# One decoder layer on one core: the order of the last steps of attention, the last block's queries, and the adds of the expert sums

## The chip, the cores and the metric

The kernel runs as one program on one core of a Trainium2 chip. The metric is the device time of one execution in microseconds (us). The engines are PE (TensorE), DVE (VectorE), ACT (ScalarE), POOL (GpSimd) and SP (SyncE, which only issues DMAs here). Each engine works through its own instructions in order, and semaphores tie them together.

## The reference

Two batches of 1024 tokens of width 256 go through three sublayers, each added to the stream and layer-normalised.

```
q, k, v = x@Wq, x@Wk, x@Wv                      # 16 heads of 64, in sequences of 512
qp, kp  = exp(q@W_feat - |q|^2/2)/sqrt(128), same for k
y_t     = (qp_t . sum_{s<=t} kp_s v_s) / (qp_t . sum_{s<=t} kp_s + 1e-6)
x       = layernorm(x + y@Wo)

att     = softmax(q k / sqrt(8)) over 77 context tokens, 32 half heads of width 8
att     = att[even half] - lam * att[odd half];  x = layernorm(x + att@v)

scores  = sigmoid(x@gate_w.T); choose 2 of 4 groups, then 4 of 16 experts
w       = chosen scores / their sum * 2.5
x       = layernorm(x + sum_e w_e * down_e(silu(gate_e x) * up_e x) + shared(x))
```

## The kernel before

**Blocks.** The 2048 tokens are four blocks of 512 (`NBLK` = 4, `NT` = 4 column tiles of 128). A Python list of jobs, `schedule()`, is made once; every engine's program walks the same list and issues its own part of each job, so the list is the order of the work on every queue. `merged(main, extra)` lays a second list evenly into a first. A job that an engine has no part in costs it nothing.

**Attention.** Steps t = 0 to 67 run the linear attention, 16 heads per block (`attention_jobs`). Beside them, `chain_jobs(b, s)` puts the rest of block b's layer at s = t - 16(b+1): output projection and first norm (s = 4), queries (5), scores (7, 8), probabilities and their weighing with the context values (10 to 14, the second norm at the end of 14), transposes and gate (15), routing and the shared expert (16 to 18), scatter of the rows to their experts' regions in DRAM (19, job `dispatch`: 16 indirect DMAs that POOL issues). For the third block these steps are t = 52 to 67, the end of attention. With its dispatch come `ends` and `table` (L1272 to L1288), small DVE steps that count how many tiles of 128 rows each expert has; `pack` (L1731 to L1733, L1451) turns the result into registers' worth of numbers that SP, PE and ACT read.

**Last block.** The last block (`DENSE`) can't wait for a dispatch, so all 16 experts are computed for all of its tokens ("dense"). Its output projection, first norm, transposes (`turn stream`, L1630) and queries stand between attention and the tile loop. A query job (L1506 with `w_xq` as the stationary side) makes 128 of the 256 query columns for 512 tokens in 6 matmuls of 512 columns: 3 passes of high and low halves in f16, times 2 halves of the inner size. ACT copies the high part (L994), DVE makes the low part (L1362), and SP then moves the pieces with 12 DMAs (L748) into `xq`, whose partitions 0 to 31 hold the high part, 32 to 63 the low part and 64 to 95 the high part again for 4 half heads of each of 8 groups. A score job is one matmul of 96 partitions (L1648) and one maximum on DVE (L1367), 32 in all.

**Tile loop.** Steps 0 to 36 run 32 pairs of tiles of the other three blocks: rows in (SP, L790), transposes (`tile turn`, L1726), gate and up matmuls (`tile up`), down matmuls (`tile down`), and POOL's two scatters of the results (L907). Into each step's jobs goes a part of the last block's chain (`gaps`): scores in steps 1 to 7, the maxima in 8, 24 probability jobs and 16 weighing jobs in 9 to 16, the second norm in 17, transposes and gate in 19, routing and shared expert in 20 and 21, weights in 22. From step 24 on every second step has the jobs of one dense expert.

**A dense expert.** `dense_jobs(e)` is gate e, up e, weigh e-1, keep e-1, down e-2. In time: ACT's tanh (L1068), two DVE products (L1461, L1465), one DVE product with the weights (L1471), ACT's high part (L1073), POOL's low part (L912), PE's down matmuls. The tanh of expert e+1 waits for POOL's low part of expert e-1.

**Last stage.** The dense experts that are left are merged with 12 sums: SP fetches a token's four expert rows into one of three buffers (`fetch`, L802), and `combine` (L1484 to L1486) adds them pairwise, adds the result to the total, and takes the statistics (L1177, L1178). After four of them comes the third norm of that block (`norm3`; the rows are scaled on ACT, L1077). The last block's own totals and norm end the program.

## Time and profile before

| | us |
|---|---|
| median of 3 runs (lowest, highest) | 1026.03 (1025.96, 1027.13) |
| profiled execution, its own time | 1016.03 |
| its span, first to last instruction | 1014.0 |
| PE busy | 843.3 (83%) |
| DVE busy | 658.9 (65%) |
| ACT busy | 498.0 (49%) |
| POOL busy | 349.8 (34%) |

The span is 2.03 us shorter than the execution's own time, and that is 10.0 us (1.0%) under the median of the timed runs. Busy shares are means over stages that differ; the windows among the rows below give each stage by itself. In every view times count from the span's start, and a line's number is that of the code above.

### The profile page before, as it was taken

The numbers are of one execution on the slowest core, as the hardware profiler recorded it, in microseconds if no ns is written. First come the engines' busy times: TensorE is split into PE (matmuls) and PEld (weight loads), VectorE is DVE, ScalarE is ACT, GpSimd is POOL, SyncE is SP. The second block draws the span as 40 slices with busy tenths as digits, with TensorE's granted clock in tenths as the row PEclk, the third lists the DMA queues.
The fourth block names the chain that finished last, engine by engine and source line by source line (L and its number), as shares of the span: only waits on it lengthen the run. The fifth ranks groups of instructions, "written<-read, shape, count | busy, mean of one in ns | idle before, by whom it ended". The sixth has DMA issues, their size and how long they took to land.

```text
span 1014.0 us, 19634 instructions
## 1 busy us (share of the span) xinstructions
PE 843.3 (83%) x6908; PEld 628.4 (62%) x6908; DVE 658.9 (65%) x1714; ACT 498.0 (49%) x1003; POOL 349.8 (34%) x376
## 2 busy tenths in 40 slices
PE   5899969999789898999889889886577787699753
PEld 2578757766566676767667667665355565576432
DVE  4676644567566955776694576568366666764888
ACT  4777656344565435367443437720125763454221
POOL 4211111001781171079116105912304672355121
PEclk9999998999999999899989989987778997899986
DMA  8466666131121232011033221242533222332341
GB/s 294 106 169 185 136 129 181 34 81 33 34 54 34 64 131 58 21 32 44 22 83 114 60 78 32 73 172 95 167 91 112 79 89 68 110 99 97 122 153 75
DMA packets 70157, 96.64 MB, mean 95 GB/s; under 512 B 19632, under 2 KB 50480, under 8 KB 69552
## 3 DMA queue, kind: packets, MB, share of 16 engines
q1 hardware_dynamic: 64688, 79.92, 27.7%
q0 software_dynamic: 5376, 15.47, 4.2%
q8 instruction: 59, 0.97, 0.4%
q14 instruction: 34, 0.28, 0.1%
HBM read 42.33 MB, written 33.10 MB: 74 GB/s over the span
## 4 chain that ended last, share of the span: by engine, by line
PE 47%; DVE 24%; ACT 8%; issue 7%; POOL 6%; SPq 4%; DMA 3%; ACTq 0%; DVEq 0%
PE ps L1506 22%; PE ps L1603 4%; POOL prob L885 4%; PE ps L1606 4%; PE ps L1584 4%; PE ps L1593 3%; SPq L688 2%; PE ps L1574 2%; PE ps L1575 2%; PE ps L1576 2%; DVE xmax L1367 1%; PE ps L1563 1%; PE ps L1648 1%; POOL low_parts L878 1%; DVE st L1177 1%
## 5 line engine op out<-in xcount | busy, mean ns | idle before, releaser
L878 POOL TENSOR_TENSOR low_parts<-square,qk 128x512 f16<-128x512 f32 x64 | 76.0, 1188 | 414.3 <-DVE qk L1314 414.3
L1312 DVE SCALAR_TENSOR_TENSOR low_parts<-ps,qk 128x512 f16<-128x512 f32 x64 | 44.2, 690 | 107.6 <-ACT square L969 104.5
L885 POOL TENSOR_TENSOR prob<-prob_full,prob 128x512 f16<-128x512 f32 x84 | 101.3, 1231 | 6.1 <-ACT prob_full L1007 5.6
L964 ACT ACTIVATE qk<-ps 128x512 f16<-128x512 f32 x64 | 38.1, 596 | 131.7 <-PE ps L1506 131.7
L907 POOL DMA_INDIRECT rows_out<-attn_mem,dest x64 | 62.4, 975 | 101.3 <-ACT attn_mem L1058 86.8
L1506 PE MATMUL ps<-x_split,w_qkv 128*128 128x512 f16 x384 | 94.4, 383 | 0.9 <-DVE low_parts L1312 0.9
L1603 PE MATMUL ps<-attn_mem 128*128 128x65 f32 x512 | 92.2, 272 | 2.1 <-issue 2.1
L1603 PEld LDWEIGHTS ps<-attn_mem 128*128 128x128 f32 x512 | 80.1, 195 | 10.2 <-issue 3.3
L1606 PE MATMUL ps<-run,attn_mem 128*128 128x65 f32 x384 | 75.0, 277 | 0.0
L1584 PE MATMUL ps<-attn_mem 128*128 128x128 f32 x512 | 74.2, 291 | 0.0
L980 ACT ACTIVATE attn_mem<-ps 128x512 f32<-128x512 f32 x64 | 38.3, 599 | 70.1 <-PE ps L1576 69.4
L1584 PEld LDWEIGHTS ps<-attn_mem 128*128 128x128 f32 x512 | 67.6, 203 | 1.7 <-DVE xmax L1367 0.3
L1593 PEld LDWEIGHTS ps<-attn_mem 128*128 128x128 f32 x448 | 62.2, 203 | 9.5 <-ACT square L969 1.5
L1506 PE MATMUL ps<-xv,prob 128*128 128x68 f16 x1152 | 46.2, 195 | 21.9 <-POOL prob L885 19.0
L1506 PE MATMUL ps<-attn_mem,w_qkv 128*128 128x128 f16 x512 | 60.4, 236 | 4.3 <-DVE x_mem L1393 3.3
L900 POOL DMA_INDIRECT rows_in<-rows,slot_i x48 | 46.5, 969 | 50.5 <-DVE slot_i L1267 36.4
L1593 PE MATMUL ps<-attn_mem 128*128 128x65 f32 x448 | 61.9, 281 | 1.4 <-ACT square L969 1.2
L1007 ACT ACTIVATE prob_full<-ps 128x512 f32<-128x512 f32 x96 | 59.7, 622 | 6.1 <-POOL prob L885 4.9
L1506 PEld LDWEIGHTS ps<-xv,prob 128*128 128x128 f16 x1152 | 43.1, 99 | 30.8 <-issue 23.2
L1574 PE MATMUL ps<-qk,w_feat_high 128*128 128x512 f16 x128 | 50.3, 393 | 12.7 <-DMA qk<-low_parts 12.3
L1367 DVE TENSOR_REDUCE xmax<-ps 128x4 f32<-128x308 f32 x128 | 53.0, 469 | 10.1 <-PE ps L1648 10.1
L1606 PEld LDWEIGHTS ps<-run,attn_mem 128*128 128x128 f32 x384 | 59.0, 194 | 0.0
(284 smaller groups left out, 2122.4 us busy)
## 6 DMA issues: line engine op xcount, KB each, us to landing
qk<-low_parts SPq DMA_DIRECT2D x128, 128.0 KB, 2.4
attn_mem<-rows_in SPq DMA_DIRECT2D x64, 144.0 KB, 2.2
late_mem<-ffn_w SPq DMA_DIRECT2D x17, 384.0 KB, 3.6
rows_in<-zero_row SPq DMA_DIRECT2D x32, 144.0 KB, 2.2
up_split<-late_mem SPq DMA_DIRECT2D x16, 256.0 KB, 3.4
xq<-late_mem SPq DMA_DIRECT2D x48, 64.0 KB, 2.0
x_stage<-xT SPq DMA_DIRECT2D x4, 512.0 KB, 4.7
down_split<-late_mem SPq DMA_DIRECT2D x16, 128.0 KB, 3.6
```

What stands on the lines that cost most here:

```text
L878: pool.tensor_tensor(low_parts[:, n % 2, 1, :], square[:, n % 2, :], qk[:, n % 2, n // 2 % 2, 0, 1, :], ALU.subtract).then_inc(p_sql.sem, 1)
L885: pool.tensor_tensor(prob[:, n % RING, 1, :], prob_full[:, n % FULL, :], prob[:, n % RING, 0, :], ALU.subtract).then_inc(pr_low.sem, 1)
L900: pool.indirect_dma_start(rows_in[GROUP_OF[b]], bass.IndirectOffsetOnAxis(ap=slot_i[:, b, j:j + 1], axis=0), row_mem[:, b % 2, j // TOPK, ...
L907: pool.indirect_dma_start(rows_out[b], bass.IndirectOffsetOnAxis(ap=dest[:, i % YB, j:j + 1], axis=0), yb[:, i % YB, j, :], None).then_inc ...
L1007: act.activation(prob_full[:, n % FULL, :], bank[:, :], ACT.Exp, scale=float(XD) ** -0.5).then_inc(pr_exp.sem, 1)
L1367: dve.tensor_reduce(xmax[:, c, GH * g:GH * g + GH], bank[:, 0:GN].rearrange("p (j n) -> p j n", j=GH), AX.X, ALU.max).then_inc(sc_max.sem, 1)
L1506: ins = pe.matmul(dst, lhs(i), rhs(j), start=first and n == 0, stop=last and n == 2)
L1574: pe.matmul(bank[:, :], w_feat_high[:, :], source[:, 0, :], start=True, stop=False)
L1584: last = pe.matmul(bank[:, t], kf[:, n % 2, t], qf[:, n % 4, t], start=True, stop=True)
L1593: last = pe.matmul(bank[:, V1 * c:V1 * c + V1], kt[:, n % 2, c, :], v1[:, c, n, :], start=True, stop=True)
L1603: last = pe.matmul(o, att[:, (H * b + n) % 3, c, :], v1[:, c, n, :], start=True, stop=not before)
L1606: last = pe.matmul(o, qf[:, n % 4, P * c:P * c + P], held, start=False, stop=True)
```

## The change

1. For the third block the steps of `chain_jobs` are drawn together: the second norm goes from s = 14 to the end of 13, everything behind it one step forward, routing parts 2 and 3 and the prefix sums into one step, so dispatch, `ends` and `table` go from t = 67 to t = 65 and `pack` from behind two output projections to t = 66. The first two blocks keep their steps.
2. The first `rows in` jobs go ahead of the last block's output projection. The last block's transposes go from ahead of the loop into step 1, its queries into steps 2 to 7, mixed with the scores. POOL spreads the query weights beforehand (job `spread wxq`, t = 63, 6 copies of 128x512 f16) as high, low, high columns for each group of 4 half heads; 8 query jobs then make 96 rows each, in the layout of `xq`, and the 12 DMAs are gone. ACT copies all 96 rows, DVE subtracts on rows 32 to 63.
3. Scores of the last block run group by group. Its second norm goes to the end of step 16, transposes and gate to 18, routing and shared expert to 19 to 22, weights to 23. Dense expert 0's gate and up go into step 21, and the dense jobs from step 24 on are each one expert further.
4. Of the three adds of a `combine` the first two go from DVE to POOL; DVE waits for them.

```diff
-    if 10 <= s <= 14:
-        for n in range(6 * (s - 10), min(6 * (s - 9), CHUNKS)):
+    if 10 <= s <= 13:
+        for n in range(6 * (s - 10), 6 * (s - 9)):
...
+    tail = [weighs(b, CHUNKS - 1) + [("norm2", b, 0)],
+            several("turn cross", range(2)) + several("gate", [0]),
+            several("route", [0]) + several("shared up", range(2)) + several("route", [1]),
+            several("route", [2]) + several("shared down", range(2)),
+            several("route", [3]) + several("prefix", [0]),
+            several("dispatch", [0]) + several("keep", [0])]
+    if closing:
+        tail[-1] += [("ends", GROUP_OF[b], 0), ("table", GROUP_OF[b], 0)]
+        tail = [tail[1], tail[2], tail[3] + tail[4], tail[5], [("pack", GROUP_OF[b], 0)]]
+        if s == 13:
             jobs += weighs(b, CHUNKS - 1) + [("norm2", b, 0)]
...
+def last_chain():
...
+    gaps[1] = several("turn stream", range(2))
+    part = []
+    for g in range(NG + 1):
+        if g < NG:
+            part += several("queries", [g])
+        if g:
+            part += several("scores", range(NT * (g - 1), NT * g))
+    spread(part, 2, 6)
+    gaps[8] = several("turn maxima", [0])
...
+    spread(part + weighs(DENSE, CHUNKS - 1), 9, 8)
+    gaps[16] += several("norm2", [0])
+    gaps[18] = several("turn cross", range(2)) + several("gate", [0])
+    gaps[19] = several("route", [0]) + several("shared up", range(2))
+    gaps[20] = several("route", [1])
+    gaps[21] = several("route", [2]) + several("shared down", range(2)) + dense_jobs(0)
+    gaps[22] = several("route", [3])
+    gaps[23] = several("weights", [0])
...
-    out_parts = chain[4]
-    jobs += out_parts[:2] + [("pack", 0, 0)] + out_parts[2:]
     for step in range(-3, 0):
         jobs += tile_jobs(0, step)
-    jobs += chain[5]
+    jobs += [("project out", DENSE, n) for n in range(NT)] + [("norm1", DENSE, 0)]
...
+                elif kind == "spread wxq":
+                    pool.wait_ge(*weighed(b - 1, 2 * NG))
+                    for part in range(2):
+                        for copy in range(3):
+                            pool.tensor_copy(w_xq3[...], w_xq[...]).then_inc(wxq_spread.sem, 1)
+                elif kind == "combine":
+                    i = NT * b + n
+                    four = yg[i % YG]
+                    pool.wait_ge(*yg_loaded[i % YG](i // YG + 1, 0))
+                    pool.tensor_tensor(four[:, 0:2, :], four[:, 0:2, :], four[:, 2:4, :], ALU.add).then_inc(paired.sem, 1)
+                    pool.wait_ge(*paired(i, 1))
+                    pool.tensor_tensor(four[:, 0, :], four[:, 0, :], four[:, 1, :], ALU.add).then_inc(paired.sem, 1)
...
+                elif kind == "queries" and b == DENSE:
+                    dve.wait_ge(*xq_high(b, n + 1))
+                    dve.scalar_tensor_tensor(xq[32:64, n, :], bank[32:64, :], 1 / W_SCALE, xq[32:64, n, :], ALU.mult,
+                                             ALU.subtract).then_inc(xq_low.sem, 1)
...
-                    dve.wait_ge(*yg_loaded[i % YG](i // YG + 1, 0))
+                    dve.wait_ge(*paired(i + 1, 0))
                     four = yg[i % YG]
-                    link(dve.tensor_tensor(four[:, 0:2, :], four[:, 0:2, :], four[:, 2:4, :], ALU.add))
-                    link(dve.tensor_tensor(four[:, 0, :], four[:, 0, :], four[:, 1, :], ALU.add))
                     dve.tensor_tensor(total[:, n, :], four[:, 0, :], total[:, n, :], ALU.add).then_inc(folded.sem, 1)
```

## Rows read from the trace of the kernel before

**Rows 1.** Windows: length, busy us by engine (instructions), granted clock, DMA share, GB/s.

```profile
664.00:702.40 38.40, 26.01 (x219) 22.75 (x215) 30.73 (x102) 7.42 (x13) 0.91 (x2) 0.81 0.21 81
702.40:740.20 37.80, 20.80 (x124) 14.44 (x125) 14.87 (x52) 2.88 (x5) 15.39 (x16) 0.68 0.53 171
740.20:766.70 26.50, 25.04 (x229) 18.84 (x230) 21.68 (x52) 10.78 (x30) 4.63 (x5) 0.89 0.32 98
...
835.50:877.00 41.50, 26.29 (x248) 21.79 (x249) 30.88 (x86) 14.70 (x44) 11.36 (x12) 0.79 0.24 74
877.00:933.60 56.60, 56.52 (x509) 39.68 (x508) 33.24 (x61) 31.34 (x94) 31.41 (x33) 1.00 0.29 94
...
938.60:1010.90 72.30, 42.81 (x214) 23.09 (x213) 61.80 (x152) 16.40 (x29) 12.56 (x10) 0.82 0.31 112
```

**Rows 2.** Timeline of PE around the tile loop's start: start, us, [idle before <-releaser].

```profile
703.13 8.01 PE L1506 MATMUL ps<-w_o,yT 128*128 128x256 f16 x48 [2.71 <-DVE yT L1345]
...
721.23 1.94 PE L1630 MATMUL ps<-ident,rows 128*128 128x128 f32 x8 [4.54 <-DVE rows L1194]
724.68 4.87 PE L1506 MATMUL ps<-late_mem,w_xq 128*128 128x512 f16 x12 [1.50 <-DVE late_mem L1358]
729.38 0.60 PE L1726 MATMUL ps<-ident,attn_mem 128*128 128x128 f32 x4
740.21 0.67 PE L1648 MATMUL ps<-xk,xq 96*128 96x308 f16 x2 [10.23 <-issue]
```

**Rows 3.** Timeline of DVE from the third block's second norm on.

```profile
667.34 0.42 DVE L1177 BATCH_NORM_STATS2 st<-rows 128x6 f32<-128x256 f32 x1
...
702.22 0.17 DVE L1267 CAST slot_i<-slot_f 128x16 int32<-128x16 f32 x1
702.30 0.68 DVE L1345 TENSOR_TENSOR yT<-ps,yT 128x512 f16<-128x512 f32 x1
...
706.42 0.16 DVE L1288 TENSOR_TENSOR row_n<-row_n,tile_f 128x1 f32<-128x1 f32 x1
```

**Rows 4.** Timelines of POOL and of SP: last dispatch, rows in, queries' DMAs.

```profile
721.67 0.96 POOL L900 DMA_INDIRECT rows_in<-rows,slot_i  x1 [0.30 <-issue]
...
725.06 3.59 SPq L790 DMA_DIRECT2D attn_mem<-rows_in  x6
730.98 7.72 SPq L748 DMA_DIRECT2D xq<-late_mem  x12
```

**Rows 5.** One line's instructions: duration ns min/median/max, first and last start.

```profile
L1362 DVE SCALAR_TENSOR_TENSOR late_mem<-ps,late_mem x2: 692/692/692, 728.1 to 730.2; 128x512 f16<-128x512 f32 x2
...
L912 POOL TENSOR_TENSOR prob<-prob x16: 1147/1251/1472, 894.4 to 995.9; 128x512 f16<-128x512 f32 x16
```

**Rows 6.** Timeline of POOL: one operation with one input, one with two.

```profile
11.22 3.55 POOL L870 TENSOR_SCALAR_AFFINE_SELECT xk<-xk 128x2464 f16<-128x2464 f16 x1
...
665.25 0.46 POOL L890 TENSOR_TENSOR x_mem<-x_mem 128x128 f32<-128x128 f32 x1 [2.60 <-DVE x_mem L1393]
```

**Rows 7.** Timelines of ACT, POOL and DVE in the last stage.

```profile
943.30 0.63 ACT L1073 ACTIVATE prob<-prob 128x512 f16<-128x512 f32 x1 [3.45 <-DVE prob L1471]
...
944.01 1.33 POOL L912 TENSOR_TENSOR prob<-prob 128x512 f16<-128x512 f32 x1 [4.85 <-ACT prob L1073]
...
943.18 0.69 DVE L1484 TENSOR_TENSOR square<-square 128x512 f32<-128x512 f32 x1
943.90 0.42 DVE L1485 TENSOR_TENSOR square<-square 128x256 f32<-128x256 f32 x1
944.36 1.26 DVE L1486 TENSOR_TENSOR yT<-square,yT 128x256 f32<-128x256 f32 x1
945.65 0.43 DVE L1177 BATCH_NORM_STATS2 st<-yT 128x6 f32<-128x256 f32 x1
...
946.21 0.65 DVE L1461 SCALAR_TENSOR_TENSOR prob<-prob,ps 128x512 f32<-128x512 f32 x1
...
961.36 0.69 DVE L1461 SCALAR_TENSOR_TENSOR prob<-prob,ps 128x512 f32<-128x512 f32 x1 [2.62 <-ACT prob L1068]
```

More of the change, by code:

```diff
@@ L1 @@
+import collections
 from contextlib import ExitStack
@@ new lines, in chain_jobs, with several, spread @@
+    if closing:
+        tail[-1] += [("ends", GROUP_OF[b], 0), ("table", GROUP_OF[b], 0)]
+        tail = [tail[1], tail[2], tail[3] + tail[4], tail[5], [("pack", GROUP_OF[b], 0)]]
+        if s == 13:
+            jobs += weighs(b, CHUNKS - 1) + [("norm2", b, 0)]
+    if 14 <= s < 14 + len(tail):
+        jobs += tail[s - 14]
+    return jobs
+def last_chain():
+    def several(kind, ns):
+        return [(kind, DENSE, n) for n in ns]
+    gaps = collections.defaultdict(list)
+    def spread(part, first, steps):
+        per = -(-len(part) // steps)
+        for i in range(steps):
+            gaps[first + i] += part[per * i:per * (i + 1)]
+    gaps[1] = several("turn stream", range(2))
[7 more added lines that the diff above has]
+    gaps[8] = several("turn maxima", [0])
+    part = []
+    for n in range(CHUNKS):
+        part += [("probs", DENSE, n)]
+        if n >= 3:
+            part += weighs(DENSE, n - 3)
+    spread(part + weighs(DENSE, CHUNKS - 1), 9, 8)
[6 more added lines that the diff above has]
+    gaps[23] = several("weights", [0])
+    return gaps
@@ L191, in schedule @@
             jobs.append(("experts", 0, 1))
-    chain = {step: chain_jobs(DENSE, step) for step in range(4, 19)}
-    out_parts = chain[4]
-    jobs += out_parts[:2] + [("pack", 0, 0)] + out_parts[2:]
+            jobs.append(("spread wxq", DENSE, 0))
     for step in range(-3, 0):
         jobs += tile_jobs(0, step)
-    jobs += chain[5]
-    gaps = {}
-    def spread(parts, first, steps):
-        part = [j for p in parts for j in p]
-        per = -(-len(part) // steps)
-        for i in range(steps):
-            gaps[first + i] = part[per * i:per * (i + 1)]
-    spread([chain[7], chain[8]], 1, 7)
-    gaps[8] = chain[9]
-    spread([chain[step] for step in range(10, 15)], 9, 9)
-    for i, step in enumerate((15, 16, 17, 18)):
-        gaps[19 + i] = chain[step]
-    dense = [dense_jobs(e) for e in range(NE + 2)]
-    done = 0
+    jobs += [("project out", DENSE, n) for n in range(NT)] + [("norm1", DENSE, 0)]
+    gaps = last_chain()
+    done = 1
     for step in range(0, PAIRS_OF[0] + DOWN + 1):
-        extra = gaps.pop(step, [])
-        if step >= 23 and step % 2 == 0:
-            extra = extra + dense[done]
+        extra = gaps[step]
+        if step >= 24 and step % 2 == 0:
+            extra = extra + dense_jobs(done)
             done += 1
@@ L226, in schedule @@
             ahead[i + 2].append(("norm3", bb, 0))
-    rest = [job for part in dense[done:] for job in part]
+    rest = [job for e in range(done, NE + 2) for job in dense_jobs(e)]
     jobs += merged(rest, [job for part in ahead for job in part])
@@ L742, in _ @@
                         load_context(b // BLK_PER_BATCH)
-                elif kind == "queries" and n == KD - 1:
+                elif kind == "queries" and b != DENSE and n == KD - 1:
                     sp.wait_ge(*xq_high(b, KD))
```

47 lines of the change are left out of this document (27 added, 20 removed).

## The prediction

> **What bounds the kernel now.** I read the windows by stage first, then the timelines at the stages' edges, then single lines. The windows' edges are: the third block's last weighing, its slots ready, step 1 of the tile loop, step 8, the last block's second norm, step 24, the last scatter landed, the first sum fetched, the end. In [rows 1] each stage has its own bound. 664 to 702: DVE, 30.7 of 38.4 us busy. 702 to 740: nothing, PE works 20.8 of 37.8 us at a granted clock of 0.68; the largest gap is 10.23 us before the first score [rows 2], in which SP takes 7.72 us to issue the queries' DMAs [rows 4]. 740 to 767, steps 1 to 7: PE, 25.0 of 26.5. 835 to 877: DVE, 30.9 of 41.5. 877 to 934: PE, 56.5 of 56.6. The last 72.3 us: DVE, 61.8. POOL has 12.6 us of work there, which invites the move of two adds. Whether they may go depends on what stands around them in POOL's and DVE's queues, and that is where I expect the change to lose.
>
> **Third block's chain.** The second norm starts at 667.34 [rows 3], when POOL's last add on the stream is through, issued at 665.25 [rows 6] and followed by a second of the same kind. Moved into t = 61 it still needs this add, and the weighing in front needs POOL's low parts as before. Only one head's output, 0.75 us of DVE, no longer stands ahead of it, and the weighing moves little, as PE puts that head's matmuls between its two halves: the norm begins about 1.1 us sooner. Against that, POOL now makes its six weight copies at once behind that add. No copy is in the trace. Below: 0.5 us each. Above: 1.25, the two-input low part of 512 columns (L912, median [rows 5]). I take 0.75, by the nearest one-input row, 3.55 us for 2464 columns [rows 6], with some start cost: 4.5 us, on an idle POOL. They cost DVE about 1 us where they collide with the norm's small two-input steps (the collision is shown below). So the norm ends when it did. From there to the slots (702.22) DVE keeps the same routing, but work of t = 65 and 66 falls behind them: a state, an output, another output, a transpose's low part, 2.9 us; work of t = 62 comes in, 2.1 us. Net the slots come at about 701.4, 0.8 us sooner, in a range of 3 sooner to 1 later.
>
> Behind the slots the order turns against the last block. Today the table's 3.5 us of small steps (to 706.42) lie under the output projection, which started at 703.13 [rows 2, 3]. Now they stand in DVE's queue before the last head's output, `pack` and the last transposes. From the slots on: state 0.7, low part 0.7, output 0.75, `ends` 0.15, table 3.65, output 0.75, `pack` 0.3, transposes on PE 0.7, ACT's copy 0.6, low part 0.7, together 9.0. The projection starts at 710.4 instead of 703.1 and runs to 724.0 (13.6 as before: 703.13 to 716.7, the 4.54 idle before 721.23 taken off it [rows 2]). The norm behind it takes those 4.5 us: 728.5.
>
> **Tiles from the end of attention.** POOL's 16 dispatches end at 722.6 today and the rows are fetched at 725.06 [rows 4]; they move with the slots, to 724.3, and the first tile can be turned at about 726.9. Step 1 is then at 727.8 instead of 740.7, and the 10.23 us gap is gone. Late next is the first query: transposes 728.6 to 730.5, ACT's and DVE's parts to 731.8.
>
> **Queries made in place.** Eight jobs of 6 matmuls instead of two, none outside the loop. 12 matmuls took 4.87 us at the low clock level [rows 2]; at the high one a 512-column matmul is half, 0.216, so a job is 1.3 us and eight are 10.4. DVE pays 8 x 0.6 (L1362 spans 0.69 [rows 5] and overlaps the next by a tenth), ACT 8 x 0.6. SP loses 7.7 us of issues. This work lies in steps 2 to 7, where PE is full: its 25.0 us of steps 1 to 7 [rows 1] less one turn, plus 10.4, is 34.3. DVE there has 21.7 + 4.8 = 26.5, so it doesn't bind. With 2 us of waits for the ACT-DVE handover of each query and for the clock after the idle, step 8 begins at 731.8 + 36.3 = 768.1. It began at 766.7: **+1.4 us**. Ends: without those waits and with slots 2 us sooner -2.6; with 1.2 us of handover exposed at each query and the low clock for the first two, +8.
>
> **Steps 8 to 24.** Steps 8 to 16 are the same. The norm at the end of step 16 waits for the same POOL add, while DVE's 2.1 us of step 17, done in that wait today, fall behind it. DVE bounds until step 24 and gets 1.3 us more for dense expert 0. Against these 3.4 us stand its 10.6 us idle of 41.5 [rows 1], of which the wider spread and a filled PE may return some 3: **+0.5**, from -3 to +4.
>
> **Steps 24 to 36.** PE is full, and one expert's selection (0.3) and down matmuls (12 x 0.11) join: **+1.6**, from 0 to +2.
>
> **Two adds on POOL.** On DVE they cost 0.72 + 0.46 per sum, start to start, and the third with its statistics 0.46 + 0.56 [rows 7]: 2.2 us x 12 = 26.4. The trace also shows why it is dearer: L1486 started at 944.36 under POOL's low part (944.01 to 945.34) and took 1.26 instead of 0.43 [rows 7]. Eight or nine of the 12 sums meet this once, +0.83 each: 33.5 in all. DVE further waits 2.62 twice for ACT, which scales rows for the norm (961.36 is one [rows 7]), 0.5 for a fetch, and has one expert (three products, 2.0) more to do than after the change, as that one has moved into step 21 to 36: 41.2 us.
>
> After: POOL's two adds. No 512-column f32 add is in the trace. Below: DVE's own 0.69 + 0.42; above: twice the 1.33 of [rows 7]. I take 1.2 + 0.7 + the handover 0.1 = 2.0, from the low part (512 columns) and the 0.46 for 128 columns [rows 6]. The merge gives DVE this order: up 8, weigh 7, sum 0, up 9, weigh 8, sum 1, up 10, sum 2, weigh 9, sum 3, up 11, norm, weigh 10, sum 4, up 12, weigh 11, sum 5, up 13, sum 6, weigh 12, sum 7, norm, up 14, weigh 13, sum 8, up 15, weigh 14, sum 9, weigh 15, sum 10, sum 11. POOL has: low part 7, adds 0, low part 8, adds 1 and 2, low part 9, adds 3, low part 10, adds 4 and 5, low part 11, adds 6, low part 12, adds 7, low part 13, adds 8 and 9, low part 14, adds 10, low part 15, adds 11. So for sums 1, 3, 4, 7 and 8 DVE has just made the product from which ACT makes the high part (0.63 + 0.1), from which POOL makes the low part (1.15 at its shortest [rows 5], + 0.1), and only then POOL adds (2.0): DVE stands still 3.9 us, with the next expert queued behind it and PE behind that. The waits: 2.0, 3.9, 0, 3.9, 5.2 (the ACT scaling sits in front), 0, 0, 3.8, 3.8, 0, 2.1, 2.6 = 27.3. At four of the sums that follow, POOL has begun the next operation when DVE's add is released: 1.1 each, 4.4. One wait for a tanh, 1.5. The third adds and statistics, 12.0. Sum 45.2 against 41.2: **+4.0**, from 0 (adds of 1.6, no collisions) to +7. The fetches stay covered: a buffer is free some 10 us before its next use, a load took 5.0 (933.6 to 938.6, two edges of [rows 1]).
>
> In a sentence the rest can do without: the Trainium skill, SBUF — State Buffer, "SBUF: two separate sides", calls the ports that DVE and POOL share an exclusive lock that the operation that starts first keeps to its end; the trace agrees (1.26 against 0.43), but by that rule DVE's add may also win the race at the four places, which would take 3.3 us off the sum. And its GPSIMD Engine Reference, "Elementwise — side-by-side cycle accounting", gives 4497 ns for an add of 2048 f32 columns on GpSimd; an estimate from that page is 1.7 us for both adds, by which the last stage would be +2.2 instead of +4.0.
>
> **The sum.** 1.4 + 0.5 + 1.6 + 4.0 = +7.5 us on the profiled execution's 1016.03 (span 1014.0 and 2.03 around it), so 1023.5 there. The timed median is 10.0 above that execution; I carry the difference over: 1026.03 + 7.5 = 1033.5.
>
> **Rivals.**
> - *The front pays.* If the slots come 4 us sooner (DVE's gaps in its 38.4 us close) or the table's steps slip into waits, the first query is at 726 and step 8 at 762, -4.6; routing spread wider gives -2.5; +1.6; the last stage at its lower half +1.5. Together -4, 1022. For it: 7.7 us DVE idle in the first window [rows 1] and the gap of 10.23. Against: the slots hang on POOL's add and a serial routing.
> - *DVE is freed.* If DVE reached its adds late enough that POOL had always finished, 26.4 + 7.1 would shrink to 12: the stage would fall onto the dense experts' own cycle, about -10, in all -6.5, 1019.5. Against: the order of the two queues above. It is the faster side's cheapest case and turns on that one point.
> - *The loop gets latency-bound.* Each query in steps 2 to 7 passes PE, ACT, DVE and then scores, and the DVE chain of the tiles shares the queue. If 1.2 us shows for each query, the low clock stays for two, and the middle gives +3: +14, 1040.
> - *It cancels,* within 2 us: every term near its lower end but none below.
>
> **Chances.** Forecast (+2 to +11) 0.50, front pays 0.12, DVE freed 0.10, latency-bound 0.20, cancels 0.08. The measurement can tell 0.2%, 2 us: faster 0.22, same 0.08, slower 0.70. The likeliest case by itself reaches from 1028 to 1037; with half of the faster cases and most of the slow one the range is 1021 to 1041.
>
> **What would show it.** After the change: POOL's six copies right behind the last stream add and under 6 us together; slots at 699 to 703; output projection at 708 to 712; the DMAs of L748 gone for the last block and no PE gap over 4 us before the first score; 8 query jobs of 1.3 us; step 8 at 764 to 772; in the last stage DVE's waits before its one add in two kinds, near 4 us and near nothing, released by POOL; L1486 at 1.26 where POOL works. I am wrong if those waits sum to less than 15 us, or if step 8 comes before 762.

## The result, and the profile after

The changed kernel took 1032.56 us (median of 11 runs, 1025.53 to 1037.57); the kernel before took 1024.05 in the same rounds (median of 11, 1017.63 to 1028.58). The ratio is 1.0081, 95% interval 1.005 to 1.0112: slower by 8.3 us, from 5.1 to 11.5. The forecast was 1033.5, +7.5. Here and below medians are over all executions, while ratios and intervals leave out those more than 1.5% above the fastest of the same kernel; e2's profile (1032.79) is of one that they leave out.

The profiled execution took 1032.56, its span is 1030.5, against 1016.03 and 1014.0. These 16.5 us are not all the change's: 9.7 of them are there before any changed instruction runs (the last block's attention begins at 522.1 instead of 512.4, with the same code in front of it; in e1 to e4, with that code too, it begins at 512.3 to 522.8). From that point on the span is 6.9 us longer, and that is what the rows below divide.

Windows of the changed kernel, with the stages' own edges (columns as in [rows 1]): the second norm of the third block to its slots; slots to step 1; steps 1 to 7; steps 8 to 16; steps 17 to 23; steps 24 to 36; the first sum's load; the last stage.

```profile
671.60:709.85 38.25, 27.97 (x210) 24.35 (x209) 29.45 (x95) 7.91 (x14) 3.56 (x7) 0.76 0.19 73
709.85:737.17 27.32, 19.70 (x136) 16.90 (x136) 14.22 (x57) 1.19 (x2) 15.54 (x16) 0.75 0.59 202
737.17:777.71 40.54, 35.63 (x282) 24.66 (x281) 30.70 (x64) 16.71 (x40) 5.80 (x6) 0.93 0.28 81
777.71:843.10 65.39, 47.80 (x625) 37.50 (x623) 40.31 (x76) 44.31 (x116) 39.62 (x44) 0.91 0.26 79
843.10:890.71 47.61, 34.91 (x321) 26.76 (x319) 34.55 (x97) 17.50 (x55) 15.09 (x16) 0.87 0.26 80
890.71:948.72 58.01, 57.94 (x516) 40.34 (x514) 34.29 (x61) 31.74 (x95) 32.71 (x33) 1.00 0.27 89
948.72:953.88 5.16, 4.79 (x27) 2.47 (x26) 1.97 (x3) 1.23 (x2) 1.62 (x2) 1.00 0.81 289
953.88:1030.50 76.62, 40.17 (x187) 21.05 (x187) 41.25 (x125) 15.24 (x27) 32.92 (x33) 0.75 0.31 111
```

Three of the stages of the kernel before, cut at the same events (slots to step 8, steps 8 to 16, steps 17 to 23), and its last stage from the first fetch's issue on:

```profile
702.39:766.65 64.26, 45.79 (x353) 33.23 (x354) 36.51 (x105) 13.65 (x35) 19.97 (x21) 0.77 0.44 141
766.65:830.94 64.29, 47.52 (x625) 37.64 (x623) 40.79 (x77) 44.57 (x116) 39.77 (x45) 0.92 0.29 89
830.94:877.04 46.10, 30.72 (x303) 25.40 (x300) 33.73 (x94) 16.87 (x50) 15.28 (x18) 0.81 0.26 79
933.67:1013.99 80.32, 47.50 (x240) 25.47 (x238) 63.79 (x155) 17.63 (x31) 13.95 (x11) 0.82 0.35 125
```

Slots to step 8 takes 27.3 + 40.5 = 67.9 instead of 64.3; steps 8 to 16, 65.4 instead of 64.3; 17 to 23, 47.6 instead of 46.1; 24 to 36, 58.0 instead of 56.6; the last stage 5.2 + 76.6 = 81.8 instead of 80.3, although DVE is busy in it for 43.2 us instead of 63.8.

PE at the loop's start, to be laid beside [rows 2], and POOL's weight copies:

```profile
719.29 12.14 PE L1555 MATMUL ps<-w_o,yT 128*128 128x256 f16 x96 [1.50 <-DVE yT L1392]
735.72 0.81 PE L1785 MATMUL ps<-ident,attn_mem 128*128 128x128 f32 x4 [4.29 <-DMA attn_mem<-rows_in]
...
740.69 2.76 PE L1555 MATMUL ps<-late_mem,prob 128*96 128x512 f16 x12 [1.61 <-DVE late_mem L1405]
```

```profile
671.78 3.39 POOL L944 COPY prob<-w_xq 128x512 f16<-128x512 f16 x6
```

The projection starts 9.50 us behind the slots (709.79) instead of 0.74, the 10.23 us gap before the first score has become one of 1.61 before the first query, and the first two query jobs, 12 matmuls, are 2.8 us of PE. In the last stage, POOL's queue and DVE's:

```profile
952.77 1.15 POOL L956 TENSOR_TENSOR prob<-prob 128x512 f16<-128x512 f32 x1 [3.54 <-ACT prob L1120]
953.88 1.27 POOL L951 TENSOR_TENSOR x_stage<-x_stage 128x512 f32<-128x512 f32 x1
955.23 0.72 POOL L953 TENSOR_TENSOR x_stage<-x_stage 128x256 f32<-128x256 f32 x1
959.86 1.15 POOL L956 TENSOR_TENSOR prob<-prob 128x512 f16<-128x512 f32 x1 [3.91 <-ACT prob L1120]
960.97 1.26 POOL L951 TENSOR_TENSOR square<-square 128x512 f32<-128x512 f32 x1
962.31 0.73 POOL L953 TENSOR_TENSOR square<-square 128x256 f32<-128x256 f32 x1
963.00 1.26 POOL L951 TENSOR_TENSOR low_parts<-low_parts 128x512 f32<-128x512 f32 x1
```

```profile
958.44 0.68 DVE L1522 TENSOR_TENSOR prob<-prob,ps 128x512 f32<-128x512 f32 x1
963.08 1.47 DVE L1535 TENSOR_TENSOR yT<-square,yT 128x256 f32<-128x256 f32 x1 [3.96 <-POOL square L953]
...
966.50 0.42 DVE L1535 TENSOR_TENSOR yT<-low_parts,yT 128x256 f32<-128x256 f32 x1
...
972.13 0.42 DVE L1535 TENSOR_TENSOR yT<-x_stage,yT 128x256 f32<-128x256 f32 x1 [3.95 <-POOL x_stage L953]
```

Read the two queues together. DVE ends its product at 959.12, ACT makes the high part of it (0.6), POOL the low part from 959.86 to 961.01, and only then come the two adds, to 963.04; DVE had nothing else to do. POOL makes the adds of sum 2 right behind (to 965.13), and DVE, which comes to that sum at 966.50, takes it without a wait. Over the stage, who waited for whom (us, times, longest):

```profile
DVE yT L1535 <- POOL square L953: 15.2, 4, 5.4
DVE yT L1535 <- POOL x_stage L953: 8.3, 3, 4.0
DVE yT L1535 <- POOL low_parts L953: 5.5, 3, 4.0
```

### The profile page after: what moved, and what is told of

Read it like the earlier page. It is cut to its first block, busy times and chain, and to the rows that moved or that the text cites. A ratio compares the mean times of both kernels' runs of the same rounds, so it can differ in the third digit from the quotient of the medians.

```text
span 1030.5 us, 19735 instructions
## 1 busy us (share of the span) xinstructions
PE 860.9 (84%) x6944; PEld 637.0 (62%) x6944; DVE 644.9 (63%) x1696; ACT 501.5 (49%) x1009; POOL 376.0 (36%) x406
## 4 chain that ended last, share of the span: by engine, by line
PE 46%; DVE 22%; POOL 11%; ACT 8%; issue 6%; SPq 5%; DMA 2%; ACTq 0%; POOLq 0%; DVEq 0%
PE ps L1555 22%; PE ps L1652 4%; POOL prob L915 4%; PE ps L1655 4%; PE ps L1633 3%; SPq L718 3%; PE ps L1642 3%; DVE xmax L1418 2%; PE ps L1623 2%; PE ps L1624 2%; PE ps L1625 2%; POOL rows_in L930 1%; PE ps L1612 1%; POOL low_parts L908 1%; POOL prob L956 1%
## 5 line engine op out<-in xcount | busy, mean ns | idle before, releaser
L1652 PE MATMUL ps<-attn_mem 128*128 128x65 f32 x512 | 96.6, 282 | 2.3 <-issue 2.1
L1555 PE MATMUL ps<-x_split,w_qkv 128*128 128x512 f16 x384 | 97.3, 391 | 1.0 <-DVE low_parts L1359 1.0
L1655 PE MATMUL ps<-run,attn_mem 128*128 128x65 f32 x384 | 78.4, 288 | 0.0
L1633 PE MATMUL ps<-attn_mem 128*128 128x128 f32 x512 | 71.8, 284 | 0.0
L1024 ACT ACTIVATE attn_mem<-ps 128x512 f32<-128x512 f32 x64 | 38.3, 599 | 68.7 <-PE ps L1625 67.9
L1555 PE MATMUL ps<-xv,prob 128*128 128x68 f16 x1152 | 47.3, 198 | 27.3 <-POOL prob L915 25.6
L930 POOL DMA_INDIRECT rows_in<-rows,slot_i x48 | 46.7, 972 | 48.9 <-DVE slot_i L1314 34.9
L1642 PE MATMUL ps<-attn_mem 128*128 128x65 f32 x448 | 61.7, 280 | 1.4 <-ACT square L1013 1.2
L1655 PEld LDWEIGHTS ps<-run,attn_mem 128*128 128x128 f32 x384 | 62.4, 204 | 0.0
L1623 PE MATMUL ps<-qk,w_feat_high 128*128 128x512 f16 x128 | 50.3, 393 | 13.6 <-DMA qk<-low_parts 13.2
L1555 PE MATMUL ps<-w_qkv,x_split 128*128 128x512 f16 x192 | 51.7, 417 | 11.1 <-DVE w_qkv L1150 11.1
```

Source lines behind the costliest of these rows:

```text
L930: pool.indirect_dma_start(rows_in[GROUP_OF[b]], bass.IndirectOffsetOnAxis(ap=slot_i[:, b, j:j + 1], axis=0), row_mem[:, b % 2, j // TOPK, ...
L1555: ins = pe.matmul(dst, lhs(i), rhs(j), start=first and n == 0, stop=last and n == 2)
L1623: pe.matmul(bank[:, :], w_feat_high[:, :], source[:, 0, :], start=True, stop=False)
L1633: last = pe.matmul(bank[:, t], kf[:, n % 2, t], qf[:, n % 4, t], start=True, stop=True)
L1642: last = pe.matmul(bank[:, V1 * c:V1 * c + V1], kt[:, n % 2, c, :], v1[:, c, n, :], start=True, stop=True)
L1652: last = pe.matmul(o, att[:, (H * b + n) % 3, c, :], v1[:, c, n, :], start=True, stop=not before)
```

## The experiments

Twelve runs in three sets of four. A set ran on one chip with its own runs of the kernel before: median 1021.32 in the first, 1063.12 in the second, 1061.88 in the third. So ratios are compared, and stages only between profiles of like chips. "Slots to step 8" and the like are lengths between the same events in every kernel.

**e1, the adds on DVE again.**

```diff
 # POOL: kind "combine" removed; DVE, kind "combine":
-                    dve.wait_ge(*paired(i + 1, 0))
+                    dve.wait_ge(*yg_loaded[i % YG](i // YG + 1, 0))
                     four = yg[i % YG]
+                    link(dve.tensor_tensor(four[:, 0:2, :], four[:, 0:2, :], four[:, 2:4, :], ALU.add))
+                    link(dve.tensor_tensor(four[:, 0, :], four[:, 0, :], four[:, 1, :], ALU.add))
```

> The changed kernel with all three adds of a sum back on DVE, everything else as changed. Theory (POOL's adds stand behind the low parts and DVE waits for them: 27 us of waits against 26 us of adds and collisions saved): the last stage, from the first fetch's issue to the end, goes back from 81.8 to about 80 us, so this kernel is 1 to 3 us faster than the changed one and still 5 to 8 us slower than the kernel before. Rival (the POOL adds are the main loss): it comes back to within 2 us of the kernel before. Rival (they do free DVE): it is 3 us or more slower than the changed kernel.

Measured: 1019.71, ratio 0.9993 (0.9958 to 1.0028). The whole loss is gone with the adds: not the theory but its first rival, the adds as the main loss, held, and the last stage took 73.3 us where about 80 were expected. Windows of its last stage, the first sum's load and the rest up to DVE's last norm:

```profile
941.27:945.94 4.67, 4.43 (x26) 2.37 (x25) 1.98 (x4) 1.23 (x2) 1.13 (x2) 1.00 0.80 281
945.94:1011.43 65.49, 37.23 (x188) 19.82 (x187) 58.04 (x149) 15.24 (x27) 11.12 (x9) 0.80 0.35 124
```

From the first add to the end of DVE's work: 65.5 us here, 73.5 in the changed kernel (953.88 to 1027.41), 72.3 before (938.59 to 1010.86). DVE's busy time and its gaps of over 0.3 us in the three: 58.0 and 2.8; 41.3 and 28.2; 61.8 and 5.7. So the adds on POOL save DVE 16.8 us of work and cost it 25.4 of waiting, +8.0 with the gaps below 0.3 us counted too. And the other edit that reaches this stage, one expert moved out of it, is worth 6.8, not the 2.0 of its three products alone. Besides them DVE has two stretched operations fewer (an add, 1.26 instead of 0.42, and a norm step, 1.00 instead of 0.16; 1.7 together) and 2.9 us less of gaps.

**e2, the two adds one place earlier in the merge.**

```diff
-        ahead[i + 2].append(("combine", bb, c))
-        if c == NT - 1:
-            ahead[i + 2].append(("norm3", bb, 0))
+        ahead[i + 2].append(("pair", bb, c))
+        ahead[i + 3].append(("combine", bb, c))
+        if c == NT - 1:
+            ahead[i + 3].append(("norm3", bb, 0))
```

> The changed kernel, but DVE's part of each sum is put one sum later in the list than POOL's two adds, so that POOL has finished when DVE comes to it. Same work on every engine. Theory (the order of the two queues costs it, not the adds' length): DVE's waits for POOL in the last stage fall from 29 us to under 6, and the stage falls from 81.8 us by 10 to 16, to the cycle of a dense expert (4.7 us) or PE. The kernel is then 2 to 8 us faster than the kernel before. Rival (POOL's adds collide with DVE and delay the low parts, whatever the order): the stage falls by less than 4 us.

Measured: 1029.94, ratio 1.0052 (1.0009 to 1.0094). By the medians, 1029.94 and 1021.32, it would be 1.0084. Last stage 78.1 instead of 81.8: 3.7 us, where the theory wanted 10 to 16 and its rival less than 4, so this run alone speaks for the rival. DVE still waits 19.0 us for POOL (under 6 expected), and now for ACT as well:

```profile
DVE yT L1536 <- POOL square L954: 10.7, 3, 5.4
DVE prob L1513 <- ACT prob L1116: 8.8, 4, 3.0
DVE yT L1536 <- POOL x_stage L954: 7.0, 2, 4.0
```

One place in the merged list moved most pairs from one side of DVE's jobs to the other, but not past the low part in POOL's queue. e7 does that.

**e3, the last block's queries by DMA again** (the two 128-column jobs, placed by SP, all of them ahead of step 2, and scores in steps 4 to 7).

```diff
-    part = []
-    for g in range(NG + 1):
-        if g < NG:
-            part += several("queries", [g])
-        if g:
-            part += several("scores", range(NT * (g - 1), NT * g))
-    spread(part, 2, 6)
+    gaps[1] += several("queries", range(KD))
+    spread(several("scores", range(NT * NG)), 4, 4)
```

> The changed kernel with the last block's queries made as before (2 jobs of 6 matmuls, 12 DMAs by SP), now in step 1 of the tile loop, and the 32 scores in steps 4 to 7; no weight copies on POOL. Theory (PE is full in steps 2 to 7, and the 36 added matmuls cost 7.8 us there one for one): PE's busy time up to step 8 falls by 7 to 8 us, the DMAs hide behind tile work in steps 2 and 3, and step 8 begins 4 to 7 us sooner than in the changed kernel; the kernel is 4 to 7 us faster than the changed one. Rival (the DMA way's 10 us gap was the cost, the matmuls fill idle time): PE stands still 5 us or more before the first score, and the kernel is no faster than the changed one.

Measured: 1031.29, ratio 1.008 (1.0046 to 1.0113), as the change. Slots to step 8: 67.1 (711.46 to 778.59) against 67.9. The DMA's way is still there, 8.0 us of issues from 747.0 on SP. What PE waited for in steps 0 to 7:

```profile
PE ps L1684 <- DMA xq<-late_mem: 7.4, 1, 7.4
```

PE works 5.2 us less than in the change (50.2 of 67.1 against 55.4 of 67.9), and stands 7.4 us in one gap instead. So the rival held: step 8 came 0.8 us sooner behind the slots, not 4 to 7. Making the queries in place gained nothing by itself.

**e4, the table and pack behind the first part of the projection's stage.**

```diff
-        tail[-1] += [("ends", GROUP_OF[b], 0), ("table", GROUP_OF[b], 0)]
-        tail = [tail[1], tail[2], tail[3] + tail[4], tail[5], [("pack", GROUP_OF[b], 0)]]
+        tail[-1] += [("ends", GROUP_OF[b], 0)]
+        tail = [tail[1], tail[2], tail[3] + tail[4], tail[5]]
...
+    jobs += [("table", 0, 0)] + [("project out", DENSE, n) for n in range(2)] + [("pack", 0, 0)]
     for step in range(-3, 0):
         jobs += tile_jobs(0, step)
-    jobs += [("project out", DENSE, n) for n in range(NT)] + [("norm1", DENSE, 0)]
+    jobs += [("project out", DENSE, n) for n in range(2, NT)] + [("norm1", DENSE, 0)]
```

> The changed kernel with the tile table computed behind the last head's output and the last transposes (beside the output projection, where it was before), the rest of the third block's chain as changed. Theory: the output projection starts 4 to 4.5 us sooner, but the first tiles still wait for the dispatched rows and stand ahead of the last block's transposes in PE's queue, so the first query starts only 0 to 1.5 us sooner; total 0 to 2 us faster than the changed kernel. Rival (the projection's late start is what delays the queries): first query and end are 4 us sooner.

Measured: 1033.04, ratio 1.0119 (1.0079 to 1.016). The projection started 8.4 us behind the slots instead of 9.5, 1.1 sooner where 4 to 4.5 were expected, and PE then stood for the first rows, so that the first query came 30.8 us behind the slots instead of 30.9:

```profile
735.19 1.09 PE L1786 MATMUL ps<-ident,attn_mem 128*128 128x128 f32 x4 [4.91 <-DMA attn_mem<-rows_in]
```

The table is not what holds the projection; the last head's output and transposes, which the drawn-together chain leaves behind the slots, are. That this run is 0.4% above the change is within the two intervals and not explained by its stages (slots to step 8 is 66.5), and I leave it open.

**e5, adds on DVE and the third block's chain as before** (on the second chip).

```diff
 # closing block: "ends" and "table" stay behind "keep", nothing else is drawn together
-        tail = [tail[1], tail[2], tail[3] + tail[4], tail[5], [("pack", GROUP_OF[b], 0)]]
-        if s == 13:
-            jobs += weighs(b, CHUNKS - 1) + [("norm2", b, 0)]
...
+    jobs += [("project out", DENSE, n) for n in range(2)] + [("pack", 0, 0)]
+    jobs += [("project out", DENSE, n) for n in range(2, NT)]
     for step in range(-3, 0):
         jobs += tile_jobs(0, step)
-    jobs += [("project out", DENSE, n) for n in range(NT)] + [("norm1", DENSE, 0)]
+    jobs += [("norm1", DENSE, 0)]
```

> The changed kernel with the two adds on DVE again (as in e1) and the third block's chain as it was: its last weighing and second norm in t = 62, nothing drawn together, the table's steps right behind the slots and the output projection behind them, with pack after its second part. Against e1 it tells what drawing the chain together cost or gave. My theory: the projection starts 1 to 2 us behind the slots instead of 9.5, tile turn 0 still waits for the dispatches (26 us behind the slots), so the first query is some 6 to 8 us sooner, but PE is then full from step 2: slots to step 8 in 60 to 65 us against 68.6 in e1 and 67.9 in the change. Slots up to 2 us later than in e1 by the schedule, which is inside the spread of this stretch between executions (188 to 195 us from the start of the last block's attention). In all 2 to 6 us faster than e1, ratio to before 0.994 to 0.998. Rival (the early third chain is what pays, the late projection is covered): slots to step 8 stays at 67 to 69 and the ratio is 1.000 or above.

Measured: 1054.68 against 1063.12, ratio 0.9924 (0.9896 to 0.9953). Faster than the kernel before. But slots to step 8 took 74.8 us in its profile, not the 60 to 65 of the theory: its projection took 27.1 us (see e8). On one chip with the changed kernel it ran as e11.

**e6, the kernel before with the expert moved alone.**

```diff
+    gaps[21] = gaps[21] + dense_jobs(0)
...
-    done = 0
+    done = 1
```

> The kernel before with one edit of the change alone: dense expert 0's gate and up products in step 21, and each of the following one place sooner, so that the last stage has one expert less. e1's last stage took 73.3 us from the first fetch's issue against 80.3 before, of which I had ascribed 2.0 to the expert. My theory now: all 7 come from the expert and its waits for ACT, so the last stage is 73 to 74 here too; steps 17 to 24 +1.5, steps 24 to 36 +1.4; in all 3 to 5 us faster than before, ratio 0.995 to 0.997. Rival (the 7 us come from elsewhere in the change, the expert itself is worth its 2.0 us of DVE): last stage 78, in all +1, ratio 1.001.

Measured: 1057.28, ratio 0.9959 (0.9926 to 0.9993). Windows of steps 17 to 23, steps 24 to 36 and the last stage, and the same of the kernel before on this chip (e8):

```profile
870.47:920.60 50.13, 35.98 (x322) 27.25 (x319) 36.24 (x98) 18.32 (x56) 15.33 (x18) 0.86 0.26 80
920.60:978.10 57.50, 57.18 (x516) 40.27 (x514) 33.42 (x59) 30.76 (x91) 32.45 (x33) 1.00 0.26 86
978.10:1052.15 74.05, 44.47 (x215) 23.18 (x213) 60.51 (x152) 16.46 (x29) 12.61 (x10) 0.75 0.38 135
```

```profile
731.64:809.87 78.23, 50.62 (x352) 34.31 (x353) 36.30 (x104) 13.79 (x35) 19.85 (x21) 0.72 0.37 116
...
873.68:920.41 46.73, 30.52 (x304) 25.20 (x302) 33.53 (x93) 16.34 (x49) 15.10 (x18) 0.82 0.26 77
920.41:978.76 58.35, 57.83 (x509) 39.77 (x508) 33.37 (x61) 31.28 (x95) 31.48 (x33) 1.00 0.28 91
978.76:1058.82 80.06, 48.04 (x240) 25.74 (x238) 64.06 (x155) 17.63 (x31) 13.67 (x11) 0.79 0.35 125
```

+3.4 where the expert goes in, -0.9 in the full steps, -6.0 at the end: -3.5 us, against -4.4 (-0.7 to -7.9) by the ratio. The theory holds in the last stage (74.05; 73 to 74 expected) and in the total. It does not in the two stages between, where +1.5 and +1.4 were expected. In steps 17 to 23 DVE's busy time grew by 2.7 us, and PE's longest wait for the routing fell from 8.2 us to 2.9: part of the expert's work went into that wait, and which engine hands the rest on is not shown.

**e7, POOL's adds ahead of the low part.** A pair is put ahead of the last dense keep in the list, but never ahead of the sum before it.

```diff
+def with_pairs(jobs):
+    out = []
+    for job in jobs:
+        if job[0] == "combine":
+            at = len(out)
+            keeps = [i for i, j in enumerate(out) if j[0] == "dense keep"]
+            if keeps and ("fetch", job[1], job[2]) in out[:keeps[-1]]:
+                at = keeps[-1]
+            prev = [i for i, j in enumerate(out) if j[0] in ("pair", "combine")]
+            at = max(at, prev[-1] + 1 if prev else 0)
+            out.insert(at, ("pair", job[1], job[2]))
+        out.append(job)
+    return out
```

> The change with POOL's two adds of a sum put ahead of the dense low part that stands before that sum in POOL's queue (ahead of it and never ahead of the sum before), instead of behind it. My theory: the adds cost because they stand behind a low part that waits for DVE's own product and ACT; with the place changed POOL adds while DVE makes the product, DVE's waits of 3.9 us go, and the low part, 2 us later, has slack, as PE uses it a whole expert later. Last stage from the first fetch's issue 62 to 70 us against 81.8 in the change and 73.3 with the adds on DVE; ratio to before 0.988 to 0.997. Rival (the adds are dear in any place, by the length of POOL's operations and the collisions with DVE's): 74 to 80 us, ratio 1.001 to 1.008.

Measured: 1058.91, ratio 0.994 (0.9905 to 0.9975); last stage 75.3 us. The changed kernel has 81.8 and 82.0 in its two profiles, the adds on DVE 73.3 to 73.6 in theirs. So the place in POOL's queue is 6.6 of the 8.5 us. The direction of my theory held and the ratio is in its range; its 62 to 70 for the stage did not hold, and 75.3 is in the range of the rival (74 to 80), by which the adds are dear in any place. What DVE waited for from the first add on, and the longest wait of ACT's tanh in the stage:

```profile
DVE prob L1527 <- ACT prob L1130: 9.5, 5, 3.0
DVE yT L1550 <- POOL x_stage L968: 5.0, 2, 2.8
DVE yT L1550 <- POOL low_parts L968: 3.9, 2, 2.7
```

```profile
1011.76 0.60 ACT L1130 ACTIVATE prob<-ps 128x512 f32<-128x512 f32 x1 [5.25 <-POOL prob L971]
```

The low part has no slack, because a tanh writes the buffer that the low part of the expert two before it reads, and waits for that low part. All eight tanhs of the stage were released by POOL's low part, here as in the changed kernel and in e1. The theory looked at PE alone. What stands before the low part comes back as DVE's wait for ACT. PE's waits for the low part are no shorter either: 22.1 us here, 22.6 in the changed kernel, 17.8 in e1. And six of DVE's own adds fell under a POOL operation and took 0.80 to 1.47 us instead of 0.42, 5.3 us in all, where the changed kernel loses 2.0 that way. So both hold in part: the place is most of the price, and in the better place collisions and the tanh's wait take their share. A third buffer for the tanh, which would give the low part its slack, was not run.

**e8, the kernel before again**, for a second profile of it, on the second chip.

> The kernel before once more, for a second profile of it: how far the anchors of unchanged code move between executions. Expected: the start of the last block's attention between 512 and 523 us, attention's start to the slots 186 to 194, slots to step 8 within 1 us of 64.3, step 8 to 24 within 2 us of 110.4, steps 24 to the first fetch's issue within 0.5 of 56.6, the last stage within 0.5 of 80.3.

Measured: 1060.87, span 1058.8. The last stage is 80.1 and steps 8 to 24 110.5, as expected. Steps 24 to 36 took 58.4 (56.1 to 57.1 expected), and the last block's attention began at 528.4 (512 to 523). Slots to step 8 is 78.2, 14 us outside what I expected, and attention's start to the slots 203.3 instead of 186 to 194. The timeline of PE shows where the 14 us are:

```profile
732.38 8.20 PE L1506 MATMUL ps<-w_o,yT 128*128 128x256 f16 x48 [2.70 <-DVE yT L1345]
...
743.20 0.28 PE L1506 MATMUL ps<-w_o,yT 128*128 128x256 f16 x1 [1.00 <-issue]
743.92 0.27 PE L1506 MATMUL ps<-w_o,yT 128*128 128x256 f16 x1 [0.44 <-issue]
745.34 0.38 PE L1506 MATMUL ps<-w_o,yT 128*128 128x256 f16 x1 [1.15 <-issue]
...
754.57 5.08 PE L1506 MATMUL ps<-w_o,yT 128*128 128x256 f16 x27 [0.34 <-issue]
```

In the first half the matmuls run back to back; then each comes by itself, with PE waiting for nothing that the profile shows. The 96 take 27.3 us; they took 13.6 in the first profile. Such gaps, of over 0.3 us each, stand in all eight profiles of the second and third chip, 11 to 23 us behind the slots, wherever the projection is by then. Where it starts 0.7 us behind the slots (e5, e6, e8, e11, e12), it has 8 to 10 of them and takes 26.5 to 27.3 us. Where it starts 9.5 behind (e7, e9, e10), it has 4 or 5 and takes 20.9 to 22.0. One of e9's:

```profile
751.27 0.27 PE L1555 MATMUL ps<-w_o,yT 128*128 128x256 f16 x1 [1.75 <-issue]
```

**e9 to e12, four kernels on one chip** (the third, which behaves like the second): the change; e1's kernel; e5's kernel; and e5's with dense expert 1 ahead of step 24 too.

```diff
 # e12, on top of e5
-    gaps[23] = several("weights", [0])
+    gaps[23] = several("weights", [0]) + dense_jobs(1)
...
-    done = 1
+    done = 2
```

> The changed kernel again, on the same chip as the three that follow, so that each step from it is a comparison on one chip. Between chips the stretch from the third block's slots to tile turn 0 differed: the output projection, 96 matmuls, took 13.6 us in the first profile of before and 27.3 in its second, with 14 us of PE gaps of the kind 'issue' while the DMA share was 0.37 to 0.72. Expected: where the projection has such gaps, the change comes out better (its tiles start earlier and hide them), ratio 0.999 to 1.003; where it hasn't, 1.006 to 1.011.

> The change with the two adds on DVE, as e1, on the same chip as the change. My theory: the adds behind the low part cost 8 us, so this is 0.7 to 1.0 % faster than the change; last stage 73.3 against 81.8. Rival (part of e1's gain was the chip or the clock): under 0.4 %.

> As e5: adds on DVE and the third block's chain as before. My theory: starting the projection at once behind the slots instead of 9 us later gives back 1.5 to 5 us between slots and step 8, ratio to before 0.992 to 0.998 and 0.2 to 0.5 % below the run with the adds on DVE alone. Rival (the late projection is covered by the wait for the first rows, 26 to 28 us behind the slots either way): no difference between the two.

> e11 with dense expert 1 also ahead of step 24 (in step 23, behind the weights) and one expert less in the last stage. The first expert moved took 6.8 us off the last stage, of which 3.5 DVE's work and 2.9 waits for ACT; only 2.8 us of waits are left there. My theory: last stage -3.5 to -5 (69 to 70), steps 17 to 24 +2 to +3, steps 24 to 36 +0.5 to +1; in all 0 to -2 us, ratio 0.991 to 0.998. Rival (the last stage turns on its fetches by now): last stage above 72, 2 us slower than e11.

| | us | ratio to before | slots to step 8 | steps 8-16 | 17-23 | 24-36 | last stage |
|---|---|---|---|---|---|---|---|
| before (profile: e8's, second chip) | 1061.88 | 1 | 78.2 | 63.8 | 46.7 | 58.4 | 80.1 |
| e9, the change | 1064.35 | 1.0018 (0.9991 to 1.0046) | 76.9 | 65.3 | 49.6 | 58.2 | 82.0 |
| e10, adds on DVE | 1057.29 | 0.9959 (0.993 to 0.9988) | 76.9 | 65.1 | 49.6 | 58.1 | 73.6 |
| e11, and old front | 1055.29 | 0.9935 (0.9911 to 0.9959) | 74.4 | 64.6 | 49.6 | 58.1 | 73.4 |
| e12, and expert 1 | 1067.57 | 1.0041 (1.0015 to 1.0067) | 73.9 | 64.2 | 57.4 | 60.2 | 73.6 |

The windows behind the first column of stages and the last, of e9 and of e11:

```profile
732.58:809.48 76.90, 59.45 (x416) 42.63 (x416) 44.51 (x121) 17.57 (x42) 21.40 (x22) 0.84 0.35 115
...
982.64:1064.62 81.98, 42.74 (x214) 22.73 (x213) 43.27 (x128) 16.50 (x29) 34.63 (x34) 0.77 0.35 122
```

```profile
732.64:807.03 74.39, 56.98 (x388) 37.65 (x389) 41.58 (x110) 16.93 (x41) 21.31 (x22) 0.79 0.37 119
...
979.36:1052.74 73.38, 44.16 (x214) 23.07 (x213) 59.96 (x152) 16.47 (x29) 12.30 (x10) 0.75 0.38 136
```

From e9 to e10: 0.6% of the time, 6.3 us, by the ratios' difference; 8.4 in the stage. Where the projection has its gaps the change itself came out at 1.0018, as expected. The adds' price is confirmed on a second chip, just below the 0.7 to 1.0% that I expected for the ratio and above the rival's 0.4%. From e10 to e11: 2.5 us in the stage, 0.24% by the ratios, whose intervals overlap; the sign fits the stage and e5, the size is not resolved by times. e12 was to be up to 2 us faster than e11 and is 11 us slower by the ratios. It fell to its rival in total, but not by its fetches: its last stage has 2.1 us less of DVE work (55.9 against 58.0 busy) and 3.2 more of gaps. The row of what DVE waited for in e12's, then in e11's, last stage:

```profile
DVE prob L1504 <- ACT prob L1107: 7.6, 3, 2.6
```

```profile
DVE prob L1504 <- ACT prob L1107: 4.4, 2, 2.6
```

With one expert fewer the merge puts sums and experts together otherwise, and waits for ACT of 2.6 come back that e11 has covered. In steps 17 to 23 the expert costs 7.8 us, more than the 5.7 of PE's work it brings (2 to 3 were expected), and in steps 24 to 36 2.2 (0.5 to 1).

## Why the prediction was right

The sum was right, +7.5 against +8.3 (5.1 to 11.5), and +6.9 in the profiled pair behind the 9.7 us of unchanged code. The mechanism on which it turned, DVE standing behind POOL's queue, is shown. That the number came so near is partly luck: steps 8 to 24 were 2.1 us dearer than forecast and the last stage 2.5 cheaper, and the slots came early by an amount that other runs don't repeat. The profiled execution by itself was forecast at 1023.5 and took 1032.56. Taken back by the 9.7 us, its slots (700.1), projection (709.6) and step 8 (768.1) lie in the ranges given. One sign did not come true: PE stood 4.29 us for the first rows ahead of the first score. And the latency-bound rival was added up wrongly: its terms, 8 + 3 + 1.6 + 4.0, give +16.6, not +14. The steps of the sum:

- **The third block's chain.** POOL's six copies took 3.4 us, not 4.5, on an idle POOL. The slots came 2.3 us sooner in relation to the start of attention (187.7 instead of 190.0), by forecast 0.8. The runs do not bear this difference out: e1 to e4 have the same chain up to there and show 191.2 to 194.7. From slots to projection I had 9.0, it was 9.5. The rival in which the front pays needed slots 4 us sooner and is refuted.
- **Slots to step 8.** By forecast step 8 stood 66.7 us behind the slots, 2.4 later than before; it stood 67.9 behind, 3.7 later. Step 1 came 13.2 us sooner (215.1 us from attention's start instead of 228.3), by forecast 12.9, and steps 1 to 7 gave it back (40.5 us against 26.0): PE's work for queries that used to lie ahead of them, and what waits for the projection 9 us later. No PE gap was above 1.7 us between the first query and step 8. e3 shows that the queries in place are no gain here, and e11 against e10, one profile each, that the drawn-together chain loses 2.5 us behind the slots. The rival of latency is refuted too: PE's waits on handovers in steps 0 to 7 sum to 4.6 us, not 8 x 1.2.
- **Steps 8 to 24: +0.5 by forecast, +2.6 measured, and +4.4 in e9 against e8.** This is the term I mis-sized. I charged expert 0 with DVE's 1.3 us and set it against idle time. e6, the expert alone, cost 3.4 in steps 17 to 23, with 5.5 us of work added to PE and 2.7 to DVE, even though PE idles for a third of the stage. My reading is that a serial routing, which passes PE, ACT and DVE in turn, is lengthened by what is put into any of their queues; no run separates them. And 1.1 of the 2.6 (1.5 in e9 against e8) stand in steps 8 to 16, which I had put at nothing; why, no run shows. It lay inside the range of -3 to +4 for one pair and outside for the other.
- **Steps 24 to 36:** +1.6 by forecast, +1.4; against e8, -0.2. Its own spread in the kernel before is 56.6 to 58.4.
- **The last stage: +4.0 by forecast, +1.5.** The order of the two queues did what was said: from the first add on DVE waited 27.0 us for POOL where 27.3 were forecast, most of it at sums 1, 3, 4, 7 and 8 as reckoned, and 1.3 for a tanh (1.5). The adds took 1.26 + 0.72 and the handover 0.1, as reckoned 2.0. The collisions of DVE's add with POOL's next operation were two instead of four (1.47 and 1.36, where 0.42 is free): before two others POOL had itself waited for the fetch, 1.3 and 1.4 us. That is 2.4 of the 2.5 that the term was too high.

On the third chip the same kernel is at 1.0018, which the measurement does not tell from no change. Nothing in its steps 24 and later differs (its last stage is +1.9 there); what differs most is the projection, 27.3 us in the kernel before and 22.0 in the changed one. That is 13.7 and 9.8 more than in the first pair, of which slots to step 8 pays 14.0 and 9.0. So the change hides next to nothing of the disturbed projection; it starts it later, and the projection meets fewer of the gaps. I had not reckoned with that, and "slower" is shown for the first measurement alone.

In a sentence the rest can do without: the Trainium skill, SBUF — State Buffer, "SBUF: two separate sides", says that of a DVE operation with two SBUF inputs and a GpSimd operation that reads SBUF whichever starts first keeps the shared ports to its instruction's end; this trace agrees in both directions, as DVE's add took 1.47 under POOL's and one of POOL's took 1.45 instead of 1.26 where DVE's came first.

**What the change is worth by parts** (profile, us, + is slower): adds on POOL +8.0 to +8.4; third chain drawn together +2.5 behind the slots; queries in place about 0; expert 0 moved -3.5 in all; tiles from the end of attention, not run alone. What remains in e11, tiles from the end of attention, queries in place and the expert on the old front, is the version that beats both kernels, 0.9935 of the kernel before (and 1055.29 us against the change's 1064.35 on the same chip): 3.8 us less between slots and step 8 on chips where the projection is disturbed, 3.3 in the loop and the last stage. On a chip of the first kind it was not run.

## What to carry to other kernels

Work moved to an idle engine is priced by what stands ahead of it in that engine's queue, not by its duration: here 2 us of adds became 4 us of DVE standing still, because ahead of them stood an operation that DVE's own last product had to release. And read the idle share of a stage with its chain: a third of PE idle in a serial stage hid 2.1 of the 5.5 us of PE's work that e6 added and none of the 5.7 that e12 added. In e12's last stage 2.1 us less of DVE's work bought nothing, as the waits grew by 3.2.

## What the runs showed of the hardware that was not expected

- The same program took 1021 to 1024 us (medians) beside the result and in the first set, and 1062 to 1063 on two other chips. In the profiles 14 us of it lie in one stretch of 96 matmuls (13.6 against 27.3 us), in which single matmuls came with 0.34 to 2.44 us of idle before them and the releaser "issue", while in the good profile they ran back to back at a higher DMA share (0.80 in that stretch, against 0.72 and then 0.37). 25 more lie in the attention ahead of it: 178 to 189.5 and 190 to 203.3 us, with DVE, ACT and POOL equally busy and 7.9 us more of PE. What holds PE's issue is not settled by any run here. The granted clock did not start the gaps: it was 1.00 from 742 to 744, where they begin, 0.75 in the next 2 us and 0.50 from 746 to 755.
- POOL's two-input f32 add took 1.26 us for 512 columns and 0.72 for 256; that is 2.1 ns a column and 0.18 us for each instruction.
- A DVE add of 0.42 us took 1.26 to 1.47 under a POOL operation in every kernel, six to eight times in a last stage with the adds on DVE, twice in the changed kernel.
